# Value products three loop steps behind the scores, a third probability buffer, and a rewritten tail, in an attention and expert kernel on one core

## The chip, the core and the metric

The kernel runs on one core of one Trainium2 chip. The metric is the time on the device in microseconds (us) of one execution of the program. Engines are called by the names of the profile: PE (TensorE matmuls), PEld (its weight loads), DVE (VectorE), ACT (ScalarE), POOL (GpSimd) and SP (SyncE, which here only starts transfers).

## The reference, cut to what matters

Two sequences of 1024 tokens of 256 numbers pass through a cross attention with 16 heads over 64 keys and then through a mixture of 16 experts of which each token takes two, with a capacity of 320 rows for an expert.

```python
x = x + tanh(g_xattn) * attention(layernorm(x), ctx, ...)   # q@k, mask, softmax over 64 keys, @v, @Wo + bo
x = x + tanh(g_ffn) * experts(layernorm(x), gate_w, w1, w2)

# inside experts, for 2048 tokens:
probs = sigmoid(xf @ gate_w.T);  top_vals, sel = top_k(probs, 2)
weights = top_vals / (top_vals.sum(-1, keepdims=True) + 1e-06)
ranks = running count of each expert, token by token, minus 1
slot = where(ranks < 320, sel * 320 + ranks, none)          # rows past the capacity are dropped
h = gelu(padded @ w1[e]);  out_rows = h @ w2[e]             # one expert after the other
out = sum over the two choices of out_rows[slot] * weight
```

The count runs over all tokens in order, so the last tile's rows can be placed only when every tile before it has been counted, and the experts begin only when all rows are placed.

## The kernel before, in words

The program is written out by hand for each engine: five instruction streams, which meet at semaphores. An engine runs its own stream strictly in the written order, so an instruction that waits holds all behind it.

There are three parts. First the weights are prepared: the key side is folded into the query weights and the value side into the output weights, through a list of jobs (`JOBS`), of which the last eight make the folded value weights. Then comes the loop over 16 tiles of 128 tokens, 0 to 15. Last come the 16 experts.

The loop is a software pipeline (`steps`, from s = -2 to 15). In one step s, PE does in this order:

- it turns (transposes) the probabilities of tile s-2 into the PSUM tile `ps_pT` (`turn_probs`, L1217)
- it makes the scores of tile s in two halves (`score`, L1234 and L1240)
- it turns the residual rows of tile s-3 (`turn_x1`, L1248)
- it makes the value products of tile s-2, 24 matmuls into `ps_out` (`attend`, L1269), with the router's product of tile s-3 in the middle (`router`, L1256)
- in every second step it makes the counts of a pair of tiles (`counts`, L1283 to L1286), and while there are tiles left it turns the normalised input two tiles ahead (L1326).

Around it, DVE takes the row minima of the scores, subtracts them ("centres" the first eight heads, L937), sums the exponentials, makes the low part of the turned probabilities (L848, in the tail L968), adds the residual (L873, in the tail L978), and does the routing: sigmoid, the two largest, their places, the counts and the slot of each row (`slot_row`, L879, in the tail L1023). ACT makes the exponentials (L636, L640), the high part of the turned probabilities (L606), copies the turned residual rows (L622), scales the rows that are sent to the experts (`second_rows`, L615) and makes the gate's exponentials (`gate_exp`, L630). POOL splits the normalised input (L483, L484), normalises the probabilities (L492), makes the second layer norm's factor of a tile (`second_norm`, L468 to L470) and sends each tile's rows to their slots by two indirect transfers (`dispatch`, L460).

A pair r is tiles 2r and 2r+1, so pairs 5, 6 and 7 are tiles 10 to 15. Behind the last loop step all engines go through a tail that is written out tile by tile. There PE runs dummy matmuls at four places (`keep_busy`, L1193): 5 and 3 between attention work, and 40 ahead of the first expert's turned rows (L1354) and 8 behind them. When POOL has sent the last rows it writes `sent` (L540), and SP, once all transfers of rows have landed (L369), fetches the first expert's rows (L378).

Of the kernel before, what the change touches and what calls it, by code (L numbers as in the profile page):

```python
# [19 lines left out]
TILES = TOKENS // P  # L20
PER_BATCH = SEQ // P
# [54 lines left out]
def build(nc, x, ctx_in, mask, g_xattn, g_ffn, ln_gamma, ln_beta, wq, wkv, wo, bo, gate_w, w1, w2, out):  # L76
# [8 lines left out]
    with ExitStack() as held:  # L85
# [65 lines left out]
        probs = sb("probs", [P, 2, HEADS, KEYS])  # L151
# [5 lines left out]
        kv_rows = probs[:, :, :, :].rearrange("p a n k -> p a (n k)")  # L157
# [4 lines left out]
        l2 = sb("l2", [P, 2, 3])  # L162
        eps_c = sb("eps_c", [P, 1])
# [63 lines left out]
        ps_attn = ps_out[:, 0:DIM]  # L227
# [36 lines left out]
        gated_read = sem("gated_read")  # L264
# [26 lines left out]
        JOBS_AFTER = {-2: range(N_FIRST, N_FIRST + 4), -1: range(N_FIRST + 4, N_KEYS + 4), 0: range(N_KEYS + 4, N_JOBS)}  # L291
# [10 lines left out]
        LAST = TILES - 1  # L302
        LATE_PAIR = PAIRS - 3
        CONSTS = 7
# [97 lines left out]
        def _(pool):  # L402
# [60 lines left out]
            def second_norm(t):  # L463

                p = t % 2
                pool.wait_ge(stats2_ready, t + 1)
                wait(pool, z2_ready, t - 1)
                done.done(pool.tensor_tensor(l2[:, p, 0:1], mv2[:, p, 1:2], eps_c[:, :], ALU.add))  # L468
                done.done(pool.tensor_tensor(l2[:, p, 1:2], l2[:, p, 0:1], power[:, 0:1], ALU.pow))
                pool.tensor_scalar(l2[:, p, 2:3], mv2[:, p, 0:1], l2[:, p, 1:2], -1.0, ALU.mult, ALU.mult).then_inc(ln2_ready, 1)  # L470

            def step(s, j, i):
# [14 lines left out]
                def normalise():  # L487

                    t, p = s - 1, (j + 1) % 2
                    if exists(t):  # L490
                        pool.wait_ge(norm_ready, t + 1)
                        pool.tensor_tensor(probs[:, p], probs[:, p], norm[:, p, :, None].to_broadcast([P, HEADS, KEYS]),  # L492
                                           ALU.mult).then_inc(normed, 1)

                if 1 <= s <= 2:
                    normalise()
                    split()
                else:
                    split()
                    if exists(s - 3) and s < LAST:  # L500
                        second_norm(s - 3)
                    normalise()
                    if s == LAST:
                        second_norm(s - 3)
# [6 lines left out]
                r = i - 3  # L511
                if exists(r, PAIRS) and s < LAST:
                    if j == 0:
# [4 lines left out]
                    dispatch(r, j)  # L518
                    if s == LAST - 1:
                        dispatch(r, 1)  # L520
# [3 lines left out]
            mark_tokens(PAIRS - 3)  # L524
            pool.wait_ge(slots_ready, PAIRS - 2)
# [35 lines left out]
        def _(act):  # L561
# [82 lines left out]
            def step(s, j, i):  # L644
# [29 lines left out]
                if exists(s):  # L674
                    probs_exp(s)
# [767 lines left out]
```

## Time and profile before

| quantity | value |
|---|---|
| time, median of 3 runs | 340.29 us (338.02 to 340.69) |
| the profiled execution: its own time | 339.9 us |
| the profiled execution: its span | 338.2 us |
| mean granted TensorE clock | 0.968 of full speed |
| PE busy | 308.3 us, 91% |
| DVE, ACT, POOL busy | 251.2, 207.9, 191.4 us |
| PE: value products (L1269) | 384 matmuls, 289 ns each by the mean |
| POOL: indirect transfers of rows (L460) | 32, 1043 ns each |

The span is the time from the first to the last instruction of the profiled execution; 1.7 us of its own time lie outside. In a timeline row, the number behind the start is how long the engine was busy with the group of instructions, and the brackets at its end say how long the engine had been idle ahead of it and what ended that. A busy PE is not a PE at its peak: a matmul's busy time overlaps with the next one's, so the pace is read from the distance of starts. The loop lies between about 33 and 156 us of the span, the tail of the attention part between 156 and 178, the experts from 186 to the end.

### The profile page before, as it was taken

To read this page: it belongs to the slowest core of one execution; us is meant where nothing else is said; L and a number is where in the kernel's file an instruction comes from. 1 tells how busy PE (TensorE), PEld (TensorE's weight loads), DVE (VectorE), ACT (ScalarE), POOL (GpSimd) and SP (SyncE) were. 2 spreads that over 40 slices of the span, in tenths; PEclk is the share of its full clock that TensorE was granted. 3 is DMA by queue.
4 is the path that set the end of the run, shared out by engine and by line. 5 is a ranking of instruction groups with operands and counts; after the bars stand their busy time and mean duration, and the time that the engine had idled before them with its cause. 6 is when DMAs were issued, how large, how long until landed. Compare 5 with 4: busy or idle time off the path is not lost. (4 is left out here: it accounts for less than half of the span.)

```text
span 338.2 us, 6265 instructions
## 1 busy us (share of the span) xinstructions
PE 308.3 (91%) x2077; PEld 267.3 (79%) x2080; DVE 251.2 (74%) x585; ACT 207.9 (61%) x570; POOL 191.4 (57%) x242
## 2 busy tenths in 40 slices
PE   8989999999999999998849999999999999999800
PEld 3646779988888888887724899999999999999700
DVE  2679887698989898989755398888888888887200
ACT  2646877887888888866461376666666666665300
POOL 8034566585777777788771023555555555566650
PEclk9999999999999999999978999999999999999965
DMA  6989999700111111111224737878787878853440
GB/s 159 274 241 292 182 167 152 195 19 16 49 49 55 57 57 64 56 51 62 78 95 149 249 104 201 204 205 208 204 216 211 224 202 220 211 82 43 48 46 8
DMA packets 40906, 45.68 MB, mean 135 GB/s; under 512 B 5461, under 2 KB 34666, under 8 KB 40874
## 3 DMA queue, kind: packets, MB, share of 16 engines
q1 hardware_dynamic: 33410, 35.78, 39.3%
q0 software_dynamic: 7424, 9.48, 15.6%
q8 instruction: 17, 0.28, 0.4%
q14 instruction: 15, 0.12, 0.2%
q10 hardware_dynamic: 40, 0.02, 0.0%
HBM read 28.02 MB, written 17.24 MB: 134 GB/s over the span
## 5 line engine op out<-in xcount | busy, mean ns | idle before, releaser
L554 POOL DMA_INDIRECT out_dram<-wqT,diag x48 | 73.3, 1528 | 77.4 <-DMA out_dram<-wqT,diag 43.4
L1370 PE MATMUL ps_scores<-value_t,score_t 128*128 128x320 f32 x384 | 59.1, 310 | 0.0
L1370 PEld LDWEIGHTS ps_scores<-value_t,score_t 128*128 128x128 f32 x384 | 56.5, 188 | 0.4 <-DVE value_t L1079 0.3
L1269 PE MATMUL ps_out<-value_t,pT 128*128 128x256 f32 x384 | 53.3, 289 | 0.9 <-DVE pT L968 0.9
L1240 PE MATMUL ps_scores<-score_t,xn 128*128 128x512 f32 x192 | 53.9, 426 | 0.0
L1269 PEld LDWEIGHTS ps_out<-value_t,pT 128*128 128x128 f32 x384 | 47.7, 189 | 1.7 <-issue 1.6
L1240 PEld LDWEIGHTS ps_scores<-score_t,xn 128*128 128x128 f32 x192 | 36.4, 190 | 6.8
L713 ACT ACTIVATE ps_scores<-ps_scores 128x640 f32<-128x640 f32 x30 | 20.6, 688 | 34.2 <-PE ps_scores L1370 34.1
L460 POOL DMA_INDIRECT padded<-z,slot_row x32 | 33.4, 1043 | 10.0 <-issue 7.1
L640 ACT ACTIVATE probs<-ps_scores,row_low 128x64 f32<-128x64 f32 x128 | 38.0, 327 | 0.5 <-DVE row_low L941 0.5
L1093 DVE CAST value_t<-ps_scores 128x640 fp32r<-128x640 f32 x30 | 24.7, 824 | 18.0 <-ACT ps_scores L713 17.8
L492 POOL TENSOR_TENSOR probs<-probs,norm 128x1024 f32<-128x1024 f32 x15 | 28.6, 1906 | 5.5 <-DVE norm L909 5.5
L640 ACT ACTIVATION_READ_ACCUMULATOR probs<-ps_scores,row_low 128x1 f32 x128 | 28.4, 222 | 0.0
L848 DVE TENSOR_TENSOR pT<-ps_pT,pT 128x512 fp32r<-128x512 f32 x28 | 18.5, 660 | 5.2 <-ACT pT L606 4.9
L1095 DVE TENSOR_TENSOR value_t<-ps_scores,value_t 128x512 fp32r<-128x512 f32 x30 | 20.8, 692 | 1.0
L1106 DVE TENSOR_TENSOR score_t<-raw,score_t 128x1024 fp32r<-128x1024 f32 x16 | 19.4, 1216 | 2.6 <-POOL sent L540 2.6
L1193 PE MATMUL ps_misc<-zeros 128*128 128x512 bf16 x62 | 18.8, 461 | 1.5 <-DVE zeros L805 1.2
L1079 DVE TENSOR_TENSOR value_t<-ps_pT,value_t 128x640 fp32r<-128x640 f32 x16 | 13.1, 816 | 8.2 <-ACT value_t L701 8.2
L606 ACT ACTIVATE pT<-ps_pT 128x512 fp32r<-128x512 f32 x32 | 18.0, 644 | 0.9 <-PE ps_pT L1217 0.9
L701 ACT ACTIVATE value_t<-ps_pT 128x640 fp32r<-128x640 f32 x16 | 11.3, 706 | 11.9 <-PE ps_pT L1354 11.7
L630 ACT ACTIVATE gexp<-ps_scores,l 128x16 f32<-128x16 f32 x16 | 4.4, 276 | 22.3 <-PE ps_scores L1256 16.7
L483 POOL CAST xn<-xn_full 128x256 fp32r<-128x256 f32 x16 | 6.4, 399 | 20.6 <-ACT xn_full L654 20.5
(210 smaller groups left out, 690.0 us busy)
## 6 DMA issues: line engine op xcount, KB each, us to landing
raw<-in_L_ffn_w_dram SPq DMA_DIRECT2D x16, 512.0 KB, 4.8
wo_sb<-in_L_ffn_w_dram SPq DMA_DIRECT2D x16, 512.0 KB, 3.5
padded<-empty SPq DMA_DIRECT2D x2, 2064.0 KB, 31.0
diag<-padded SPq DMA_DIRECT2D x16, 258.0 KB, 4.9
out_dram<-x SPq DMA_DIRECT2D x16, 128.0 KB, 1.7
padded<-empty SPq DMA_DIRECT2D x1, 1032.0 KB, 34.1
diag<-padded SPq DMA_DIRECT2D x16, 64.5 KB, 4.7
wq_sb<-in_L_xattn_Wq_dram SPq DMA_DIRECT2D x2, 512.0 KB, 8.0
```

The source lines that it names most:

```text
L460: pool.indirect_dma_start(padded, bass.IndirectOffsetOnAxis(ap=slot_row[:, r % 2, k, q:q + 1], axis=0), z2[:, (2 * r + k) % RING, q], None ...
L492: pool.tensor_tensor(probs[:, p], probs[:, p], norm[:, p, :, None].to_broadcast([P, HEADS, KEYS]), ALU.mult).then_inc(normed, 1)
L554: pool.indirect_dma_start(out, bass.IndirectOffsetOnAxis(ap=xg[0:SLOTS[k], r, k, TOKEN:TOKEN + 1].bitcast(U32), axis=0), y[0:SLOTS[k], j, ...
L640: op = act.activation(probs[:, j, n], ps_scores[:, 1, at:at + KEYS], ACT.Exp, scale=-1.0, bias=row_low[:, n:n + 1], accum_out=row_sum[:, j ...
L713: act.activation(h_at(t, h), ps_scores[:, 2 * h:2 * h + 2, 0:CAPACITY], ACT.Gelu).then_inc(h_act, 1)
L1093: dve.tensor_copy(h_high_of(p)[:, fs], h_at(t, h)).then_inc(h_high, 1)
L1095: dve.tensor_tensor(h_low_of(p)[:, fs], h_at(t, h)[:, :, 0:n], h_high_of(p)[:, fs, 0:n].bitcast(F32), ALU.subtract)
L1106: dve.tensor_tensor(w1_hl(p, 1), raw1[:, p], w1_hl(p, 0).bitcast(F32), ALU.subtract).then_inc(w1_low, 1)
L1193: pe.matmul(ps_misc[:, :], idle_rows[:, 0:P], idle_rows, start=True, stop=True)
L1240: op = pe.matmul(dst, xn[:, t % 2, a, c], mv, start=False, stop=last)
L1269: op = pe.matmul(ps_attn, pT[:, a, c], mv, start=c == 0 and (a, b) == PARTS[0], stop=c == HC - 1 and (a, b) == PARTS[-1])
L1370: op = pe.matmul(ps_scores[:, f, 0:CAPACITY], w1_hl(p, a)[:, c, f * P:(f + 1) * P], x_hl(p, b)[:, c], start=c == 0 and (a, b) == PARTS[0], ...
```

## The change

All work on a tile behind its scores moves one step back in the loop: probabilities of tile s-3 are turned in step s, the residual rows of tile s-4 are turned, and so on. For that `probs` has three buffers in place of two (`DEEP = 3`). The eight value jobs are spread 3, 2 and 3 over the steps -1, 0 and 1, where they were 4 and 4 over -1 and 0.

Behind the last scores, the probabilities of the next tile are turned ahead of the value products of a tile. For this the value products of tiles 13 and 15 go to `ps_misc` and not to `ps_out`, and their turned probabilities go to a part of `score_t` that is no longer read. The turned residual rows and the router's product are put between matmuls of the next tile's value products, in place of the 5 and 3 dummies. The 40 and 8 dummies ahead of the experts stay.

In the tail, the second layer norm of tiles 12 to 15 leaves POOL with the power alone; DVE adds two small instructions and ACT one per tile (`shift`). The routing step that stood in the last loop step for pair 5 is now in the tail. Two waits are loosened, so that products of tile 13 need not wait for the residual of tile 12. The core of the diff (the loop's shift by u = s-1 repeats on every engine):

```diff
-        probs = sb("probs", [P, 2, HEADS, KEYS])
+        probs = sb("probs", [P, DEEP, HEADS, KEYS])
+        pT_late = score_t[:, 6 * 1024:].rearrange("p (k c n) -> p k c n", k=2, c=HC)
-        ps_attn = ps_out[:, 0:DIM]
+        def attn_of(t):
+            return ps_misc[:, 0:DIM] if t in (LAST - 2, LAST) else ps_out[:, 0:DIM]
+        def pT_of(t, k):
+            return pT_late[:, k] if t in (LAST - 2, LAST) else pT[:, k]
...
+        VALUES_AFTER = {0: range(N_KEYS + 3, N_KEYS + 5), 1: range(N_KEYS + 5, N_JOBS)}
+        LATE_TILE = 2 * LATE_PAIR + 2
@@ GpSimd: second_norm, and the tail
+                if t >= LATE_TILE:
+                    pool.tensor_tensor(l2[:, p, 1:2], l2[:, p, 0:1], power[:, 0:1], ALU.pow).then_inc(ln2_ready, 1)
+                    return
...
             mark_tokens(PAIRS - 3)
+            normalise(LAST)
+            mark_tokens(PAIRS - 2)
             pool.wait_ge(slots_ready, PAIRS - 2)
-            dispatch(PAIRS - 3, 0, (0,))
+            dispatch(PAIRS - 3, 0)
+            second_norm(LAST - 3)
+            dispatch(PAIRS - 3, 1, (0,))
             second_norm(LAST - 2)
-            dispatch(PAIRS - 3, 0, (1,))
-            dispatch(PAIRS - 3, 1)
-            mark_tokens(PAIRS - 2)
+            dispatch(PAIRS - 3, 1, (1,))
             mark_tokens(PAIRS - 1)
             second_norm(LAST - 1)
             pool.wait_ge(slots_ready, PAIRS - 1)
             dispatch(PAIRS - 2, 0)
+            second_norm(LAST)
             dispatch(PAIRS - 2, 1)
-            second_norm(LAST)
@@ ScalarE: the tail
+            copy_probs(LAST - 2)
+            later_exp(LAST, 8, 12)
+            gate_exp(LAST - 4)
+            later_exp(LAST, 12, HEADS)
+            second_rows(LAST - 4)
             copy_probs(LAST - 1)
+            copy_x1(LAST - 3)
+            gate_exp(LAST - 3)
+            copy_probs(LAST)
+            second_rows(LAST - 3)
             copy_x1(LAST - 2)
-            second_rows(LAST - 3)
             gate_exp(LAST - 2)
             second_rows(LAST - 2)
-            copy_probs(LAST)
             copy_x1(LAST - 1)
+            gate_exp(LAST - 1)
             second_rows(LAST - 1)
-            gate_exp(LAST - 1)
@@ VectorE: the tail
+            low_probs(LAST - 2, 0)
+            low_probs(LAST - 2, 1)
             dve.wait_ge(exped0, TILES)
...
-            place(PAIRS - 3, 0, 2, PAIRS - 2)
-            first_residual(LAST - 2)
-            second_stats(LAST - 2)
+            begin(PAIRS - 3, 0, 2)
+            find(0, 2)
             dve.wait_ge(exped1, TILES)
...
-            dve.tensor_tensor(probs[:, p], probs[:, p], norm[...], ALU.mult).then_inc(normed, 1)
+            first_residual(LAST - 3)
+            link.sync()
+            choose(PAIRS - 3, 0, 2)
+            low_probs(LAST - 1, 0)
+            low_probs(LAST - 1, 1)
+            weigh(PAIRS - 3, 0, 2)
+            counts_of(PAIRS - 3)
+            place(PAIRS - 3, 0, 2, PAIRS - 2)
+            second_stats(LAST - 3)
+            first_residual(LAST - 2)
+            second_stats(LAST - 2)
+            low_probs(LAST, 0)
+            low_probs(LAST, 1)
+            first_residual(LAST - 1)
             begin(PAIRS - 2, 0, 2)
             find(0, 2)
+            second_stats(LAST - 1)
             link.sync()
             choose(PAIRS - 2, 0, 2)
...
             place(PAIRS - 2, 0, 2, PAIRS - 1)
+            first_residual(LAST)
+            second_stats(LAST)
@@ TensorE: the last step and the tail
+                if s == LAST:
+                    turn_probs(LAST - 2)
...
             turn_probs(LAST - 1)
-            turn_x1(LAST - 2)
-            keep_busy(5)
-            attend(LAST - 1, {HC // 2: lambda: router(LAST - 2)})
+            attend(LAST - 2, {1: lambda: turn_x1(LAST - 3), HC - 3: lambda: router(LAST - 3), HC - 1: lambda: counts(PAIRS - 3)})
             turn_probs(LAST)
+            attend(LAST - 1, {2: lambda: turn_x1(LAST - 2), HC - 2: lambda: router(LAST - 2)})
+            attend(LAST, {2: lambda: turn_x1(LAST - 1), HC - 2: lambda: router(LAST - 1)})
             counts(PAIRS - 2)
-            turn_x1(LAST - 1)
-            keep_busy(3)
-            attend(LAST, {HC // 2: lambda: router(LAST - 1)})
             turn_x1(LAST)
+            router(LAST)
             count_one(0)
-            router(LAST)
             count_one(1)
```

What this makes of three streams is best seen in the order of the instructions. Line numbers of the change are its own.

On TensorE, ahead of the value products of the tile behind the loop's last one, before (the products are those of tile 14, L1217 turns probabilities, L1248 residual rows):

```order
L1217 MATMUL ps_pT<-ident,probs 128x128 x8
L1248 MATMUL ps_scores<-ident,x 128x128 x2
L1193 MATMUL ps_misc<-zeros 128x512 x5
L1269 MATMUL ps_out<-value_t,pT 128x256 x12
L1256 MATMUL ps_scores<-small_t,wq_sb 128x16 x2
L1269 MATMUL ps_out<-value_t,pT 128x256 x12
L1217 MATMUL ps_pT<-ident,probs 128x128 x8
```

and in the change, from the turned probabilities of tile 14 on (L1271; L1323 are value products of tile 13, L1302 turned residual rows of tile 12, L1310 the router, L1337 and L1340 counts):

```order
L1271 MATMUL ps_pT<-ident,probs 128x128 x8
L1323 MATMUL ps_misc<-value_t,score_t 128x256 x3
L1302 MATMUL ps_scores<-ident,x 128x128 x2
L1323 MATMUL ps_misc<-value_t,score_t 128x256 x12
L1310 MATMUL ps_scores<-small_t,wq_sb 128x16 x2
L1323 MATMUL ps_misc<-value_t,score_t 128x256 x6
L1337 MATMUL ps_scores<-running,ones_b 128x16
L1340 MATMUL ps_scores<-both,before 128x16
```

The dummies are gone, and the residual rows of one tile are turned behind the first three products of the next.

On GpSimd, from the last normalised probabilities of the loop on, before (L468 to L470 are the second layer norm, first of tile 12, then of tile 13; L460 sends rows of pair 5):

```order
L492 TENSOR_TENSOR probs<-probs,norm 128x1024
L468 TENSOR_TENSOR l<-mv,eps_c 128x1
L469 TENSOR_TENSOR l<-l,power 128x1
L470 TENSOR_SCALAR l<-mv,l 128x1
L453 TENSOR_TENSOR z<-token,zeros 128x4
L460 DMA padded<-z,slot_row 32768x258
L468 TENSOR_TENSOR l<-mv,eps_c 128x1
L469 TENSOR_TENSOR l<-l,power 128x1
L470 TENSOR_SCALAR l<-mv,l 128x1
L460 DMA padded<-z,slot_row 32768x258 x3
```

and in the change (L492 normalises tile 15's probabilities, L473 sends rows of pair 5, L481 is the power of the second layer norm, of tile 12 and then of tile 13):

```order
L466 TENSOR_TENSOR z<-token,zeros 128x4
L492 TENSOR_TENSOR probs<-probs,norm 128x1024
L466 TENSOR_TENSOR z<-token,zeros 128x4
L473 DMA padded<-z,slot_row 32768x258 x2
L481 TENSOR_TENSOR l<-l,power 128x1
L473 DMA padded<-z,slot_row 32768x258
L481 TENSOR_TENSOR l<-l,power 128x1
L473 DMA padded<-z,slot_row 32768x258
```

The factor of tile 12 stood ahead of every transfer of pair 5; it now stands behind two of them.

On ScalarE in the tail, before, from the turned probabilities of tile 15 (L606) on (L622 copies the turned residual rows of tile 14, L615 scales that tile's rows, L630 is its gate):

```order
L606 ACTIVATE pT<-ps_pT 128x512 x2
L622 ACTIVATE wq_sb<-ps_scores 128x256
L615 ACTIVATE z<-x,l 128x2x256
L630 ACTIVATE gexp<-ps_scores,l 128x16
```

and in the change, from the turned probabilities of tile 14 (L625) on (L646 copies residual rows of tile 12, L654 is the gate's exponential of tile 12, then come tile 15's turned probabilities, the scaled rows of tile 12, and the residual rows of tile 13):

```order
L625 ACTIVATE pT<-ps_pT 128x512 x2
L646 ACTIVATE wq_sb<-ps_scores 128x256
L654 ACTIVATE gexp<-ps_scores,l 128x16
L625 ACTIVATE score_t<-ps_pT 128x512 x2
L635 ACTIVATE shift<-l 128x1
L639 ACTIVATE z<-x,shift,l 128x2x256
L646 ACTIVATE wq_sb<-ps_scores 128x256
```

The gate's exponential of tile 12 now stands ahead of the turned probabilities of tile 15 and of the residual rows of tile 13.

## Rows read from the trace of the kernel before

**Rows 1.** Windows: length, busy (count) of PE, PEld, DVE, ACT, POOL; clock, DMA share, GB/s.
```profile
57.00:148.00 91.00, 90.75 (x650) 81.26 (x649) 77.75 (x225) 71.82 (x284) 67.67 (x102) 1.00 0.21 61
...
174.00:178.00 4.00, 3.00 (x10) 1.11 (x11) 1.72 (x12) 3.99 (x5) 2.76 (x4) 0.50 0.29 100
```

**Rows 2.** Timeline of TensorE, the last step: start us, busy us, engine, line, operation.
```profile
144.18 0.38 PE L1248 MATMUL ps_scores<-ident,x 128*128 128x128 f32 x2
...
147.69 1.04 PE L1217 MATMUL ps_pT<-ident,probs 128*128 128x128 f32 x8
...
148.56 0.38 PE L1234 MATMUL ps_scores<-mask_b,ident_b 128*128 128x512 bf16 x1
...
151.76 0.38 PE L1248 MATMUL ps_scores<-ident,x 128*128 128x128 f32 x2
```

**Rows 3.** Timeline of the start: TensorE's one wait, then GpSimd.
```profile
47.79 0.39 PE L1234 MATMUL ps_scores<-mask_b,ident_b 128*128 128x512 bf16 x1 [0.59 <-ACT probs L640]
...
48.00 0.24 POOL L444 TENSOR_SCALAR ln_nb<-ln_a 128x4 f32<-128x4 f32 x1
...
49.87 1.91 POOL L492 TENSOR_TENSOR probs<-probs,norm 128x1024 f32<-128x1024 f32 x1 [1.63 <-DVE norm L909]
...
52.20 0.73 POOL L484 TENSOR_TENSOR xn<-xn_full,xn 128x256 fp32r<-128x256 f32 x1
```

**Rows 4.** Timeline of TensorE behind the last scores, to the first expert.
```profile
156.96 0.44 PE L1248 MATMUL ps_scores<-ident,x 128*128 128x128 f32 x2 [0.42 <-DVE x L978]
...
158.86 1.66 PE L1269 MATMUL ps_out<-value_t,pT 128*128 128x256 f32 x12 [0.39 <-DVE pT L968]
...
165.67 1.66 PE L1269 MATMUL ps_out<-value_t,pT 128*128 128x256 f32 x12 [0.47 <-DVE pT L968]
...
175.02 0.18 PE L1295 MATMUL ps_scores<-both,before 128*128 128x16 bf16 x1
...
180.12 6.21 PE L1193 MATMUL ps_misc<-zeros 128*128 128x512 bf16 x28 [0.22 <-issue]
...
186.18 0.86 PE L1354 MATMUL ps_pT<-ident,diag 128*128 128x128 f32 x6
```

**Rows 5.** Timeline of GpSimd behind the last scores.
```profile
158.23 0.57 POOL L469 TENSOR_TENSOR l<-l,power 128x1 f32<-128x1 f32 x1
...
166.70 1.06 POOL L460 DMA_INDIRECT padded<-z,slot_row  x1 [0.39 <-issue]
...
177.42 0.96 POOL L460 DMA_INDIRECT padded<-z,slot_row  x1 [0.30 <-issue]
```

**Rows 6.** Timeline of VectorE: one centring in the loop, then the tail.
```profile
144.38 0.69 DVE L937 TENSOR_TENSOR probs<-ps_scores,row_low 128x512 f32<-128x512 f32 x1
...
161.27 0.18 DVE L991 TENSOR_SCALAR gden<-gexp 128x32 f32<-128x32 f32 x1 [0.82 <-ACT gexp L630]
...
162.87 0.23 DVE L1007 TENSOR_TENSOR chosen<-iota_f,top_i 128x64 bf16<-128x64 f32 x1
...
166.01 0.16 DVE L1023 SCALAR_TENSOR_TENSOR slot_row<-top_i,rank 128x4 uint32<-128x4 uint32 x1
...
169.39 0.48 DVE L978 SCALAR_TENSOR_TENSOR x<-ps_out,tgates,x_all 128x256 f32<-128x256 f32 x1 [0.18 <-PE ps_out L1269]
...
173.20 0.21 DVE L991 TENSOR_SCALAR gden<-gexp 128x16 f32<-128x16 f32 x1 [1.14 <-ACT gexp L630]
```

**Rows 7.** Timeline of ScalarE behind the last scores.
```profile
156.86 1.13 ACT L606 ACTIVATE pT<-ps_pT 128x512 fp32r<-128x512 f32 x2
...
161.13 0.81 ACT L615 ACTIVATE z<-x,l 128x512 f32<-128x512 f32 x1
...
164.80 0.38 ACT L622 ACTIVATE wq_sb<-ps_scores 128x256 f32<-128x256 f32 x1 [0.84 <-PE ps_scores L1248]
...
172.82 0.27 ACT L630 ACTIVATE gexp<-ps_scores,l 128x16 f32<-128x16 f32 x1 [2.02 <-POOL l L470]
```

**Rows 8.** Timeline of SyncE: the first fetch of an expert's rows.
```profile
180.19 0.38 SPq L378 DMA_DIRECT2D diag<-padded  x1
```

More of the change, by code:

```diff
@@ L20 @@
 TILES = TOKENS // P
+LAST = TILES - 1
+DEEP = 3
 PER_BATCH = SEQ // P
@@ L162, in build @@
         l2 = sb("l2", [P, 2, 3])
+        shift = sb("shift", [P, 2, 1])
         eps_c = sb("eps_c", [P, 1])
@@ L499, in step @@
                     split()
[L500 to L504, printed above, removed]
+                    if exists(u - 3):
+                        second_norm(u - 3)
+                    if exists(s - 1):
+                        normalise(s - 1)
                 if s == 1:
@@ L612, in second_rows @@
                 act.wait_ge(ln2_ready, t + 1)
+                bias = l2[:, p, 2:3]
+                if t >= LATE_TILE:
+                    bias = shift[:, p]
+                    act.activation(bias, l2[:, p, 2:3], ACT.Copy, scale=l2[:, p, 1:2]).then_inc(shifted, 1)
+                    act.wait_ge(shifted, t - LATE_TILE + 1)
                 if t >= RING:
@@ L1259, in attend @@
             def attend(t, between):
-                wait(pe, x1_ready, t)
+                wait(pe, x1_ready, t if t < LAST - 2 else t - 1)
                 for c in range(HC):
@@ L1268, in attend @@
                         mv = value_w[b][:, batch_of(t), c]
-                        op = pe.matmul(ps_attn, pT[:, a, c], mv, start=c == 0 and (a, b) == PARTS[0],
+                        op = pe.matmul(attn_of(t), pT_of(t, a)[:, c], mv, start=c == 0 and (a, b) == PARTS[0],
                                        stop=c == HC - 1 and (a, b) == PARTS[-1])
@@ L1305, in step @@
                     score(s, 1)
-                if exists(s - 3):
-                    turn_x1(s - 3)
-                r = i - 2
-                counted_here = j == 1 and exists(r, PAIRS)
-                between = {}
-                if exists(s - 3):
-                    between[HC // 2] = lambda: router(s - 3)
-                if counted_here and r >= LATE_PAIR:
-                    between[HC - 2] = lambda: counts(r)
-                if exists(s - 2):
-                    attend(s - 2, between)
-                if counted_here and r < LATE_PAIR:
-                    counts(r)
+                if exists(u - 3):
+                    turn_x1(u - 3)
+                if s == LAST:
+                    turn_probs(LAST - 2)
+                if exists(u - 2):
+                    attend(u - 2, {HC // 2: lambda: router(u - 3)} if exists(u - 3) else {})
+                if ju == 1 and exists(iu - 2, PAIRS):
+                    counts(iu - 2)
                 t = s + 2
```

152 lines of the change are left out of this document (78 added, 74 removed).

## The prediction

> **What bounds the kernel now.** I read the busy shares by stretches first, to see which parts can gain at all. In the loop, from 57 to 148 us, PE is busy for 90.75 of 91 us at full clock [rows 1]. So one more step of distance between scores and products cannot shorten a loop step; it can only move work between the start, the loop and the tail. Then I read PE's timeline at both ends. At the start it has one wait, 0.59 us [rows 3]. In the tail there are two holes, filled in part by dummies: the residual rows of tile 13 are turned at 156.96 and the products of tile 14 begin at 158.86; those of tile 15 begin at 165.67 after a similar hole [rows 4]. Together that is about 4 us. Last I read what the tail's end hangs on. The last count ends on PE at 175.2; then PE runs its 40 dummies without a pause, 28 of them from 180.12 to 186.3, and the first expert's rows are turned at 186.18 [rows 4]. The transfers end at 178.38 on POOL [rows 5] and SP fetches at 180.19 [rows 8]. So two paths meet at 186.18: **the last count plus 11.1 us of dummies**, and **the last transfer plus 1.8 us plus the landing of a fetch**. The turned rows follow the dummies without a gap, so the first path decided and the second was no later. From there the experts run on PE, untouched by the change, and I take them as shifted whole.
>
> **Loop and start.** Taken out of the loop ahead of the last step is one tile's later half: turned probabilities 0.87 us (147.69 to 148.56) and residual rows, products and router 3.51 us (144.18 to 147.69) [rows 2]. The last step would begin 4.38 us earlier, at 143.3. PE is idle more at the start, though: with no products to do, it reaches the fourth tile's scores by about 50. Their split input stands on POOL behind the first norms (end 48.24), one normalisation (1.91) and the split (1.2 with its cast), thus at 50.5 to 51.4, the norms starting up to 0.9 earlier with the lighter value jobs; in the kernel before the split ended at 52.93 [rows 3]. That is 0.5 to 1.4 us of waiting where 0.59 us stood before, and the exponentials, now with less PE work to hide them, cost some tenths more. I take 0.8 us net (0 to 1.5). The last step then begins at 144.1.
>
> **The tail, link by link.** Times are estimates on the old trace's time axis. Small DVE instructions, whose rows are not shown one by one, count 0.2 us each (161.27 and 173.20 took 0.18 and 0.21) [rows 6].
>
> - PE: scores of tile 15 end at 144.1 + 0.87 + 3.20 = 148.2 [rows 2]; residual rows 0.14, turned probabilities of tile 13 0.87, products of tile 12 3.4: 152.6; turned probabilities of tile 14: 153.5.
> - DVE: in the loop the centring ends at 144.38 + 0.69, 0.9 us behind the residual rows of its step at 144.18 [rows 2, 6]; these stand at 148.2 in the last step, so it ends at 149.1. ACT: exponentials of a copy's size 0.6, copies for tile 13 1.13 [rows 7]; DVE's low parts end at 151.4. A row sum (of the centring's size, 0.7), then gate and places of pair 5, which took 161.27 to 162.87, 1.6 us [rows 6], the reciprocal and norm (0.5) and the residual of tile 12 (0.48): **154.7**. PE reached the place for tile 12's residual rows at 153.9 and waits 0.9 us.
> - PE then has 18 products and the router ahead of the counts of pair 5, of the 3.37 us that 24 and the router take [rows 2], and DVE four small instructions to their slots: 158.6.
> - POOL may now send pair 5. The order puts two transfers, 1.27 us each (0.96 busy and 0.30 of issue) [rows 5], ahead of tile 12's power (0.57): 161.9. In the old kernel even tile 13's power ended at 158.8 [rows 5], with tile 12's ahead of it.
> - ACT holds at the gate's exponential of tile 12 until then, as it did for 2.02 us at 172.82 [rows 7], and behind it in its queue stand tile 15's copies (1.1), the new `shift` (0.3 with its wait, bounded by the cheapest ACT row, 0.27, and twice that), scaled rows (0.81) and tile 13's residual rows (0.38) [rows 7]: 164.7.
> - PE reached the router of tile 13 at 161.7 and waits **3.1 us**, longer than either old hole. Rest of tile 14's products: 166.1.
> - DVE: residual and statistics of tile 14 (0.9, two of the residual's size), gate and places of pair 6 (1.6), the statistics' end (0.4, of which the two added instructions make 0.1 to 0.2 each), choice, weights and counts to slots (1.8, nine small ones): slots of pair 6 at 170.8. They were there at 166.17 [rows 6].
> - DVE goes on: residual of tile 15 begins at 171.0, against 169.39 [rows 6]; statistics until 172.3. From a tile's gate to its count took 1.82 us, 173.20 to 175.02 [rows 4, 6], and to its slots four small ones more: tile 14 until 175.0. Tile 15's gate to count 1.82: the last count ends at **177.0, against 175.2: +1.8 us**. In the old kernel a wait of 1.14 us for the gate stood in that stretch [rows 6]; it goes, since ACT has the gates in time.
> - POOL: eight transfers from 170.9 at 1.27 and one power at 0.67: end at 181.7, against 178.38: +3.3 us. Fetch at 183.5. A fetch before took under 6.0 us (180.19 to 186.18), so it lands between 186.5, if 3 us suffice, and 189.5.
>
> The first path gives 177.0 + 11.1 = 188.1, the second at most 189.5. I take the first with a tenth for the second: the experts begin at 188.2, **+2.0 us**. The profiled execution took 339.9 us by itself (span 338.2 and 1.7 around it), so its like is 341.9. The median of the runs is 0.4 above it, so I forecast **342.3 us**. Costed at nothing: the third buffer, the second homes, the loosened waits (they only allow); the DVE and POOL work of the loop, which is covered by 90.75 us of PE; the weight loads for the experts, which SP issues behind the fetches and which would be late only if the experts began much before them.
>
> **The rivals.**
>
> *The dropped clock (slower).* In the old tail PE, after a thin stretch behind the last products, ran at half clock: 0.50 in 174 to 178 [rows 1]. The old holes of about 2 us had dummies in them. The change takes these out and makes, by my sum, a hole of 3.1 us with nothing in it. If the clock falls there, the 30 products behind the hole go at half speed. Here 12 products with a busy 1.66 us follow each other at about 0.125. Dummies of 512 columns went 28 in 6.21 us at full clock, 0.22 each [rows 4]; at half clock that is 0.44, and a product of half the columns 0.22 at least. So 0.09 more for each of 30 is 2.7 us, all on the path to the last count: **345.0 us**. For: the old drop. Against: that drop came after a longer thin stretch, and work stands on both sides of this hole. The Trainium skill, "TensorE: Matmul & The Clock Gate", section "HAM oscillation — how this bites in real kernels", says that a wait between two bursts can send the next burst cold each time. By that rule 345.0 would be the sum; the old trace agrees only for the longer stretch.
>
> *The holes are filled as written (faster).* If ACT does not stand at tile 12's gate, PE saves 4 us of holes less 0.8 at the start, and DVE and POOL follow: about **337.3 us**. It decides from the point at which tile 12's power comes before about 158.5, for then the router's rows are there in time. Against: POOL's order is fixed, and the two transfers ahead of the power wait themselves for slots at 158.6.
>
> *Dummies shorter.* If the clock is up when the 40 dummies run, they take about 8.8 us and not 11.1, and the fetch decides. With a landing in 3 to 4 us that is +0.5 to +1.5: **341.3 us**. For: the clock's phase is open. Against: PE is nearly idle ahead of the dummies in the change too.
>
> *Fetch and queue late.* If the landing takes all of 6 us and the waits at each link are a tenth longer, +4: **344.3 us**.
>
> **How the numbers follow.** My case as summed, 0.46; dropped clock 0.22; shorter dummies 0.15; late fetch 0.09; filled holes 0.08. The likeliest gives 342.3, with its own range of 341.0 to 343.8 from the start's 0 to 1.5 and the fetch. The range for 8 in 10 runs from 339.2 to 345.8: it takes in all but most of the filled holes and the upper part of the clock's case. A measurement of this kernel tells about 1% from no change, 3.4 us, so faster is below 336.9 and slower above 343.7. Faster: about half of the filled holes lies below 336.9, 0.05 with rounding. Slower: nearly all of the dropped clock, half of the late fetch and a tenth of my own case, 0.31. Within 1%: 0.64.
>
> **What would show each step.** The last tile's scores should begin 3 to 4.4 us earlier; if not, the start's sum is wrong. On ACT, one gate's exponential should stand behind a wait of over 5 us for the power on POOL, and PE should wait about 3 us for copied residual rows in tile 14's products; if it waits under 1 us there, the filled holes are right. The granted clock in that stretch decides the second case. The last transfer should end about 3 us later than 178.4 and the last count about 2 us later than 175.2. If the first expert's rows are turned behind a wait, the fetch decided, and not the dummies. A loop in which PE is idle by more than some tenths would overturn all of it.

## The result and the profile after

The changed kernel takes 345.61 us by the median of 4 runs (344.20 to 346.76), beside 339.93 for the kernel before (4 runs, 338.02 to 340.69). The ratio is 1.018 with a 95% interval of 1.015 to 1.0209: 5.7 us slower by the medians and 6.1 by the ratio, where 342.3 was forecast in a range of 339.2 to 345.8. The profiled execution took 346.72 us by itself, its span is 345.0, its mean granted clock 0.956 (0.968 before). All comparisons below are ratios with their interval; they leave disturbed runs out, so they can differ from the quotient of two medians.

The loop and its two ends in windows of the profile after (length, busy time and count of PE, PEld, DVE, ACT, POOL, then granted clock, DMA share, GB/s):

```profile
27.00:57.00 30.00, 27.89 (x138) 20.81 (x137) 25.72 (x65) 21.80 (x84) 17.92 (x30) 1.00 1.12 201
57.00:148.00 91.00, 91.00 (x644) 81.11 (x643) 77.98 (x230) 72.71 (x290) 65.48 (x99) 1.00 0.15 51
163.00:165.00 2.00, 0.00 (x0) 0.00 (x0) 1.14 (x2) 1.90 (x5) 1.64 (x3) 1.00 0.27 99
...
167.00:167.50 0.50, 0.50 (x6) 0.50 (x5) 0.38 (x1) 0.50 (x1) 0.00 (x0) 1.00 0.04 8
167.50:168.00 0.50, 0.50 (x6) 0.43 (x4) 0.47 (x3) 0.17 (x1) 0.00 (x0) 0.53 0.00 0
168.00:170.50 2.50, 2.50 (x14) 2.50 (x13) 2.19 (x17) 0.38 (x1) 0.49 (x1) 0.50 0.15 52
171.00:174.00 3.00, 1.37 (x15) 1.24 (x16) 1.52 (x8) 1.27 (x3) 0.67 (x1) 1.00 0.00 0
175.00:184.00 9.00, 5.59 (x19) 2.57 (x20) 4.81 (x30) 6.54 (x9) 7.16 (x9) 0.50 0.31 108
```

The same window of the start in the kernel before:

```profile
27.00:57.00 30.00, 28.96 (x150) 22.67 (x149) 26.26 (x68) 22.40 (x82) 16.59 (x29) 1.00 1.12 192
```

In the start, 27 to 57 us, PE is idle for 2.11 us; in the kernel before it was 1.04. The loop is as full as before [rows 1]. Then come two stretches at 0.50. The second answers to the one of before; the first, with PE busy in all of it, is new. It begins at about 167.5 and ends at about 170.9.

PE's timeline of the same kernel, from the last scores to the first expert (start, busy time, engine, line, operation, and in brackets the idle time ahead and what ended it); it answers to [rows 2, 4]:

```profile
144.64 0.38 PE L1288 MATMUL ps_scores<-mask_b,ident_b 128*128 128x512 bf16 x1
...
160.79 1.67 PE L1323 MATMUL ps_out<-value_t,pT 128*128 128x256 f32 x12
165.66 0.62 PE L1310 MATMUL ps_scores<-small_t,wq_sb 128*128 128x16 f32 x4 [3.20 <-ACT wq_sb L646]
...
168.00 2.91 PE L1323 MATMUL ps_misc<-value_t,score_t 128*128 128x256 f32 x12
...
172.10 0.17 PE L1340 MATMUL ps_scores<-both,before 128*128 128x16 bf16 x1
...
179.48 0.17 PE L1349 MATMUL ps_scores<-both,before 128*128 128x16 bf16 x1
179.50 11.30 PE L1247 MATMUL ps_misc<-zeros 128*128 128x512 bf16 x40
190.64 0.86 PE L1400 MATMUL ps_pT<-ident,diag 128*128 128x128 f32 x6
```

The last scores begin 3.9 us earlier (144.64 against 148.56). The hole ahead of the router of tile 13 is 3.20 us. The 12 products at 160.79 take 1.67 us, the same 12 at 168.00 take 2.91. The last count is 4.4 us later than before, and so is the first expert: 190.64 against 186.18, again directly behind the dummies.

What held PE: ScalarE and GpSimd of the profile after, answering to [rows 5, 7].

```profile
163.06 0.27 ACT L654 ACTIVATE gexp<-ps_scores,l 128x16 f32<-128x16 f32 x1 [6.03 <-POOL l L481]
163.24 1.07 ACT L625 ACTIVATE score_t<-ps_pT 128x512 fp32r<-128x512 f32 x2
164.19 0.30 ACT L635 ACTIVATE shift<-l 128x1 f32<-128x1 f32 x1
164.53 0.81 ACT L639 ACTIVATE z<-x,shift,l 128x512 f32<-128x512 f32 x1
165.25 0.36 ACT L646 ACTIVATE wq_sb<-ps_scores 128x256 f32<-128x256 f32 x1
```

```profile
160.16 1.01 POOL L473 DMA_INDIRECT padded<-z,slot_row  x1 [2.48 <-issue]
161.47 0.96 POOL L473 DMA_INDIRECT padded<-z,slot_row  x1 [0.30 <-issue]
162.46 0.57 POOL L481 TENSOR_TENSOR l<-l,power 128x1 f32<-128x1 f32 x1
...
173.33 1.04 POOL L473 DMA_INDIRECT padded<-z,slot_row  x1 [2.76 <-DVE slot_row L1065]
...
182.81 0.96 POOL L473 DMA_INDIRECT padded<-z,slot_row  x1 [0.30 <-issue]
```

The chain is the one of the prediction: two transfers, the power, the gate behind a wait of 6.03 us, four instructions, and then PE. The last transfer ends at 183.77, 5.4 us later than before.

At the end of the run, the last three additions into the output (POOL, L571) of the changed kernel:

```profile
331.01 1.56 POOL L571 DMA_INDIRECT out_dram<-wqT,diag  x1 [2.42 <-issue]
332.87 1.56 POOL L571 DMA_INDIRECT out_dram<-wqT,diag  x1 [0.31 <-issue]
334.74 1.43 POOL L571 DMA_INDIRECT out_dram<-wqT,diag  x1 [0.30 <-issue]
```

and in the kernel before PE's last product and the first of the last three additions (L554):

```profile
320.62 0.28 PE L1399 MATMUL ps_scores<-score_t,value_t 128*128 128x256 f32 x1
324.07 1.56 POOL L554 DMA_INDIRECT out_dram<-wqT,diag  x1 [2.40 <-issue]
```

PE's last product ends at 325.7, 4.8 us later than before (320.9), but the last three additions begin 6.9 us later (331.01 against 324.07). Of the 6.8 us between the two profiled executions, 4.5 lie ahead of the first expert, 0.3 in PE's work on the experts and 2.0 in this queue. The medians differ by 5.7.

### The profile page after: what moved, and what is told of

It is laid out like the page before. It is cut to its first block and busy times, and to the rows that moved or that the text cites. A ratio compares the mean times of both kernels' runs of the same rounds, so it can differ in the third digit from the quotient of the medians.

```text
span 345.0 us, 6252 instructions
## 1 busy us (share of the span) xinstructions
PE 309.5 (90%) x2072; PEld 268.5 (78%) x2072; DVE 250.8 (73%) x592; ACT 208.8 (61%) x574; POOL 191.2 (55%) x235
## 5 line engine op out<-in xcount | busy, mean ns | idle before, releaser
L571 POOL DMA_INDIRECT out_dram<-wqT,diag x48 | 74.3, 1547 | 78.0 <-DMA out_dram<-wqT,diag 35.1
L1323 PE MATMUL ps_out<-value_t,pT 128*128 128x256 f32 x336 | 46.7, 288 | 0.0
L1323 PEld LDWEIGHTS ps_out<-value_t,pT 128*128 128x128 f32 x336 | 41.8, 189 | 0.1
L473 POOL DMA_INDIRECT padded<-z,slot_row x32 | 32.3, 1010 | 13.4 <-issue 9.2
L492 POOL TENSOR_TENSOR probs<-probs,norm 128x1024 f32<-128x1024 f32 x16 | 30.5, 1905 | 3.2 <-DVE norm L945 3.1
L666 ACT ACTIVATION_READ_ACCUMULATOR probs<-ps_scores,row_low 128x1 f32 x128 | 28.4, 222 | 0.0
L884 DVE TENSOR_TENSOR pT<-ps_pT,pT 128x512 fp32r<-128x512 f32 x26 | 17.2, 660 | 6.5 <-ACT pT L625 6.0
L654 ACT ACTIVATE gexp<-ps_scores,l 128x16 f32<-128x16 f32 x16 | 4.4, 275 | 26.9 <-PE ps_scores L1310 15.6
L736 ACT ACTIVATE value_t<-ps_pT 128x640 fp32r<-128x640 f32 x16 | 11.3, 705 | 12.5 <-PE ps_pT L1400 12.4
L1247 PE MATMUL ps_misc<-zeros 128*128 128x512 bf16 x57 | 17.4, 472 | 1.2 <-DVE zeros L840 1.2
L758 ACT ACTIVATE score_t<-raw 128x1024 fp32r<-128x1024 f32 x16 | 16.8, 1056 | 0.3
```

The costliest lines, as they stand in the source:

```text
L473: pool.indirect_dma_start(padded, bass.IndirectOffsetOnAxis(ap=slot_row[:, r % 2, k, q:q + 1], axis=0), z2[:, (2 * r + k) % RING, q], None ...
L492: pool.tensor_tensor(probs[:, p], probs[:, p], norm[:, t % 2, :, None].to_broadcast([P, HEADS, KEYS]), ALU.mult).then_inc(normed, 1)
L571: pool.indirect_dma_start(out, bass.IndirectOffsetOnAxis(ap=xg[0:SLOTS[k], r, k, TOKEN:TOKEN + 1].bitcast(U32), axis=0), y[0:SLOTS[k], j, ...
L666: op = act.activation(probs[:, t % DEEP, n], ps_scores[:, 1, at:at + KEYS], ACT.Exp, scale=-1.0, bias=row_low[:, n:n + 1], accum_out=row_s ...
L1247: pe.matmul(ps_misc[:, :], idle_rows[:, 0:P], idle_rows, start=True, stop=True)
L1323: op = pe.matmul(attn_of(t), pT_of(t, a)[:, c], mv, start=c == 0 and (a, b) == PARTS[0], stop=c == HC - 1 and (a, b) == PARTS[-1])
```

## The experiments

### The hole and the clock

**e1**, the hole filled with dummies:

```diff
-            attend(LAST - 1, {2: lambda: turn_x1(LAST - 2), HC - 2: lambda: router(LAST - 2)})
+            def fill_then_router():
+                pe.wait_ge(x1_ready, LAST - 1)
+                keep_busy(14)
+                router(LAST - 2)
+            attend(LAST - 1, {2: lambda: turn_x1(LAST - 2), HC - 2: fill_then_router})
```

> The changed kernel, with 14 dummies (3.1 us at 0.22 each) put into the 3.20 us hole in tile 14's products, ahead of the router of tile 13. Theory A (the clock fell because of the empty hole): the granted clock stays at 1.00 from 166 to 172, the products of tile 15 take 1.7 us for 12 and not 2.91, the counts of pair 6 come 1.3 us earlier and the whole is 1.3 us shorter, about 344.3. Theory B (the clock falls for another reason, or DVE's chain sets the counts anyway): the time stays at 345.6.

Measured: ratio 1.0063 (1.0043 to 1.0083), so 1.17% or 4.0 us faster than the changed kernel (2.8 to 5.2 with both intervals taken in). TensorE in e1, and two windows of it:

```profile
161.07 3.19 PE L1247 MATMUL ps_misc<-zeros 128*128 128x512 bf16 x14
164.42 0.62 PE L1310 MATMUL ps_scores<-small_t,wq_sb 128*128 128x16 f32 x4 [0.16 <-ACT wq_sb L646]
...
176.81 0.18 PE L1349 MATMUL ps_scores<-both,before 128*128 128x16 bf16 x1
176.84 10.10 PE L1247 MATMUL ps_misc<-zeros 128*128 128x512 bf16 x40
186.77 0.86 PE L1406 MATMUL ps_pT<-ident,diag 128*128 128x128 f32 x6
```

```profile
161.00:172.00 11.00, 8.87 (x63) 6.48 (x62) 6.70 (x32) 5.75 (x14) 5.23 (x9) 1.00 0.13 48
173.00:179.00 6.00, 2.42 (x10) 1.01 (x11) 4.18 (x27) 5.35 (x8) 4.60 (x6) 0.50 0.25 89
```

PE does not get on sooner, it only works at something, and the clock stays at 1.00. Theory A holds for the clock, and for its price up to the last count (1.3 expected). The whole gained more than that. The experts begin 3.87 us earlier than in the profile after. Of that, 0.5 is there at the last scores already (they begin at 144.14). Another 0.8 of it lies ahead of the router of tile 12: in the profile after, ACT stood 1.59 us between its two copies for tile 14, and here it did not. Neither of these is the work of the dummies. From the router of tile 13 to the last count it is 1.4 less (12.4 us here, 13.8 there); in e3 and e4 below, where the work at this place also ran at 1.00, it is 12.4 and 12.3. That 1.4 is the price of the dropped clock.

The last 1.2 lies in the 40 dummies, which take 9.9 us from first start to the expert, against 11.1. They begin inside the second stretch at 0.50, and 2.7 us of them lie in it here, 5.1 in the profile after. That this hangs on the hole is not shown. In e3 and e4 there is no drop behind the hole, and yet the second stretch lasts 10.2 us, as in the profile after (6.8 in e1), and the 40 dummies take 11.48 and 11.25 us up to the first expert. Their dummies, first e3, then e4 and its first expert:

```profile
174.99 11.65 PE L1247 MATMUL ps_misc<-zeros 128*128 128x512 bf16 x40
...
174.00 11.41 PE L1247 MATMUL ps_misc<-zeros 128*128 128x512 bf16 x40
185.25 0.86 PE L1400 MATMUL ps_pT<-ident,diag 128*128 128x128 f32 x6
```

**e2**, the hole made longer; **e3**, made shorter on ACT:

```diff
@@ e2, GpSimd
             dispatch(PAIRS - 3, 0)
-            second_norm(LAST - 3)
             dispatch(PAIRS - 3, 1, (0,))
+            second_norm(LAST - 3)
@@ e3, ScalarE
-            gate_exp(LAST - 3)
             copy_probs(LAST)
-            second_rows(LAST - 3)
             copy_x1(LAST - 2)
+            gate_exp(LAST - 3)
+            second_rows(LAST - 3)
```

> The changed kernel, with one more transfer (1.27 us) ahead of tile 12's power on POOL. Theory A (POOL's order holds ACT, ACT's copies hold PE): ACT waits 7.3 us at tile 12's gate and not 6.03, PE's hole is 4.5 us and not 3.20, and all that follows is 1.3 us later or, with more of the products at half clock, up to 2.3: 346.9 to 347.9. Theory B (the hole is not on the path to the end): 345.6.

Measured for e2: ratio 1.0215 (1.0175 to 1.0254), 0.35% or 1.2 us over the changed kernel's, with overlapping intervals. In its profile the first expert begins at 192.16, 1.5 us later than in the changed kernel's.

> The changed kernel, with tile 15's copies and the copy of tile 13's residual rows ahead of tile 12's gate in ACT's queue; PE's router of tile 13 still waits for that gate. Theory A: the hole ends with the gate at 163.4 and not at 165.66, so it shrinks to about 1 us, the clock stays up, and the end is 2.2 us earlier for the hole and 1.3 for the clock: 342.1. If the hole counts but the clock does not: 343.4. Theory B (neither is on the path): 345.6.

Measured for e3: ratio 1.0123 (1.0071 to 1.0175), 1.9 us faster than the changed kernel (0.2 to 3.7 by its own interval; with the changed kernel's taken in as well, from nothing to 4.0), where theory A had 3.5. Four of its six runs took 341.8 to 342.4, the other two 345.7 and 346.7; the median is 342.32. The row of the router in e2, then a window of e2:

```profile
166.31 1.04 PE L1310 MATMUL ps_scores<-small_t,wq_sb 128*128 128x16 f32 x4 [4.46 <-ACT wq_sb L646]
```

```profile
166.00:172.00 6.00, 5.69 (x26) 5.69 (x27) 2.83 (x17) 1.91 (x5) 0.25 (x1) 0.50 0.12 44
```

The hole is 4.46 us as written ahead of the run, and now the work behind it is at half clock from its first product up to 172.2. In e3, the router and a window with the hole in it:

```profile
162.61 0.59 PE L1310 MATMUL ps_scores<-small_t,wq_sb 128*128 128x16 f32 x4 [1.01 <-ACT gexp L654]
```

```profile
160.00:170.00 10.00, 7.18 (x61) 6.56 (x59) 7.08 (x34) 4.61 (x12) 6.29 (x9) 1.00 0.22 79
```

The hole is 1.01 us, where about 1 was expected, and does not lower the clock. The last count comes at 175.1 and the first expert at 186.47, 4.2 us before the changed kernel's. The direction is theory A's; the interval is too wide to tell whether the clock's part is in the time.

**e10**, the kernel before without the dummies in its holes:

```diff
-            keep_busy(5)
             attend(LAST - 1, {HC // 2: lambda: router(LAST - 2)})
...
-            keep_busy(3)
             attend(LAST, {HC // 2: lambda: router(LAST - 1)})
```

> The kernel before, without the 5 and 3 dummies in the two holes of its tail, so that two holes of about 2 us stand empty. Theory A1 (only an empty stretch as long as the changed kernel's 3.20 us drops the clock): granted clock 1.00 up to 170, no change, 339.9. Theory A2 (two holes of 2 us are enough): the clock falls to 0.50 somewhere in 159 to 170 and the products there take twice as long, 341 to 343.

Measured: ratio 1.004 (1.0009 to 1.0071). The two holes, and the windows of both:

```profile
158.11 1.66 PE L1269 MATMUL ps_out<-value_t,pT 128*128 128x256 f32 x12 [1.46 <-DVE pT L968]
...
164.92 1.67 PE L1269 MATMUL ps_out<-value_t,pT 128*128 128x256 f32 x12 [0.91 <-DVE pT L968]
```

```profile
155.00:163.00 8.00, 5.88 (x51) 5.16 (x49) 6.59 (x27) 5.07 (x17) 6.24 (x9) 1.00 0.19 66
163.00:171.00 8.00, 5.25 (x39) 4.46 (x38) 6.26 (x28) 2.07 (x5) 5.75 (x11) 1.00 0.28 99
```

The clock stays up over both, as A1 said; the time is 1.4 us longer all the same (0.3 to 2.4), which neither said. In this profile the last count ends at 174.45, the experts begin at 185.81 and PE's last product ends at 320.6, all a little earlier than before; but the last three additions begin at 325.86, 5.3 us behind PE and not 3.2. So this profile is longer at the end, and why stays open. For the granted clock, then, it was not enough that the change took dummies out; the hole it made was also longer than these two.

### The order of the tail

**e4**, tile 12's power early (DVE and POOL):

```diff
             low_probs(LAST - 1, 0)
+            second_stats(LAST - 3)
             low_probs(LAST - 1, 1)
...
-            second_stats(LAST - 3)
@@ GpSimd
+            second_norm(LAST - 3)
             pool.wait_ge(slots_ready, PAIRS - 2)
             dispatch(PAIRS - 3, 0)
-            second_norm(LAST - 3)
```

> The changed kernel, with tile 12's statistics on DVE between the two low parts of tile 14 and its power on POOL ahead of the wait for the slots of pair 5. Theory A: ACT no longer waits over 1 us at tile 12's gate, PE's hole of 3.20 us goes, the clock stays at 1.00, and the slots of pair 6 stand at about 168 and not 173; the whole is 4.5 us shorter: 341.1. Theory B (the loss of 5.7 us lies in the longer sending and the dummies, not in the hole): at most 1.5 us shorter, 344.1 or more.

Measured: ratio 1.0017 (0.9983 to 1.005), 5.5 us faster than the changed kernel. In its profile, ACT's gate of tile 12 and PE's router of tile 13:

```profile
158.78 0.28 ACT L654 ACTIVATE gexp<-ps_scores,l 128x16 f32<-128x16 f32 x1 [2.90 <-POOL l L481]
```

```profile
161.71 0.52 PE L1310 MATMUL ps_scores<-small_t,wq_sb 128*128 128x16 f32 x4
```

No hole is left in front of the router, and moving one small chain gives back all of the loss, within the interval. From the last scores to the last count the profile is 5.9 us shorter than the changed kernel's (29.1 against 35.0): 3.2 for the hole, 1.4 for the clock, 0.8 for the pause on ACT, and 0.5 in other places.

**e7** goes on from e4: tile 13's power behind two of pair 5's transfers, tile 13's residual rows copied ahead of tile 12's scaled rows, and the counts of pair 6 ahead of PE's last three products. **e11** puts DVE's gates of pair 6 ahead of tile 14's residual as well, and on PE takes tile 14's residual rows two places later and the last router behind the counts of pair 6; **e12** is e11 with 36 dummies. The part of e11 on DVE:

```diff
@@ e11 over e7, VectorE
-            first_residual(LAST - 1)
             begin(PAIRS - 2, 0, 2)
             find(0, 2)
-            second_stats(LAST - 1)
+            first_residual(LAST - 1)
             link.sync()
             choose(PAIRS - 2, 0, 2)
+            second_stats(LAST - 1)
```

> The changed kernel with the tail reordered: tile 12's statistics and power early as in the run before, tile 13's power after two of the four transfers of pair 5, the copy of tile 13's residual rows ahead of tile 12's scaled rows, and the counts of pair 6 ahead of tile 15's last three products on PE. Theory A (the tail's order alone made the loss): no hole over 1 us, slots of pair 6 at about 167 (before: 166.17), last count at about 174 and last transfer at about 178: the level of the kernel before or 1 us under it, 339 to 340. Theory B (the third step of distance costs in the loop or the start too): 341 or more.

> The reordered tail of run e7, with one more change: DVE takes the gates of pair 6 ahead of tile 14's residual (it stood idle for 1.20 us ahead of that one while the gates were ready), and PE takes tile 14's residual rows two steps later in tile 15's products, then the counts of pair 6 and last the router. Theory A (the tail's order sets the sending, and the sending the end): slots of pair 6 at 166.5 against 168.0, last transfer 1.5 us earlier, experts at about 184 since the 40 dummies stay, and 338.5 to 339.5, level with the kernel before or just under it. Theory B (PE's work after the last scores is what bounds): nothing over e7, 340.1.

> The same with 36 dummies ahead of the first expert and not 40: at 0.22 us each 0.9 us less. Theory A (the dummies end last): the experts begin 0.9 us earlier, 337.6 to 338.6. Theory B (the fetch of expert 0 ends last by then): the same time as the run before.

Measured: 1.0024 (0.9998 to 1.0051), 1.0007 (0.9967 to 1.0047) and 1.0001 (0.9961 to 1.0042). All three are level with the kernel before, none beats it. Yet in their profiles the experts begin at 184.66, 184.57 and 183.97, up to 2.2 us before [rows 4]. The last additions of e12:

```profile
326.74 1.56 POOL L570 DMA_INDIRECT out_dram<-wqT,diag  x1 [2.36 <-issue]
328.60 1.56 POOL L570 DMA_INDIRECT out_dram<-wqT,diag  x1 [0.31 <-issue]
330.47 1.43 POOL L570 DMA_INDIRECT out_dram<-wqT,diag  x1 [0.30 <-issue]
```

PE's last product ends at 319.0 there, but these begin 7.7 us later; in the kernel before it was 3.2. The queue loses this over all the experts: its first addition comes 2.2 us earlier than in the kernel before (198.45 against 200.63), its last three begin 2.7 us later. In the profiled executions, then, an earlier start of the experts is given back in that queue. How much of it in the others is open: the profiled one of e12 took 342.41 us and that of e11 342.58, where the medians of the compared runs are 339.4 and 339.5.

### Between the last count and the end

**e5** is the kernel before with `keep_busy(60)` in place of 40; **e6** is the changed kernel with `keep_busy(30)`.

> The kernel before, with 60 dummies ahead of the first expert and not 40: at 0.22 each 4.4 us more, so that the experts begin where they begin in the changed kernel (190.6). Theory A (the start of the experts passes to the end whole, and nothing else of the change is lost): 339.9 + 4.4 = 344.3, or above by what the queue of the final additions adds. Theory B (part of the start's shift is given back, or transfers already bind the experts): clearly less than 344.3, 342 or so.

> The changed kernel, with 30 dummies ahead of the first expert and not 40. The last 10 take 2.2 us at full clock. Theory A (the dummies end last by 1.8 us, the fetch of expert 0 landing 3.5 us behind its issue, at 188.8): the experts begin 1.8 us earlier, 343.8. Theory B (fetch and dummies end together): no change, 345.6. If fewer dummies leave the clock down for the first expert: 345.6 or more.

e5: ratio 1.0136 (1.0107 to 1.0165), 4.6 us over the kernel before, near the 4.4 of theory A. In the profiles the shift is smaller: its experts begin at 189.16, 3.0 us later than before and not 4.4, and its profiled execution took 342.81 us against 339.9, 2.9 more. A later start of the experts passes to the end.

e6: ratio 1.0186 (1.0138 to 1.0233), no different from the changed kernel's. But its eight executions scatter from 342.7 to 362 us, the profiled one took 356.21, and the three shortest took 342.66, 343.71 and 345.18; the middle one is at theory A's 343.8. In its profile the experts begin 2.0 us earlier than in the changed kernel's, at 188.65, behind a wait of 0.72 us for the fetch. Whether these 2.0 us reach the end stays open.

**e8** and **e9**, the kernel before and the changed one with two additions per expert and not three:

```diff
                     if k == SLOT_TILES - 1:
                         pool.wait_ge(y_last, e + 1)
+                        continue
```

(the waits for `added` count 2 * 16 in place of 3 * 16). Both leave the rows of slots 256 and up out of the output.

> The kernel before, without the third addition of each expert (the rows of slots 256 and up are left out of the output, nothing else is). The queue of the additions then has a third less to do. Theory A (this queue, and not PE, ends the run, 2.0 us behind PE's pace in the trace of before and 4.5 us in that of the change): the last addition follows PE's last product within 1.5 us, and the time falls by 2 to 4 us, to 336 to 338. Theory B (PE's pace ends the run): only the last addition itself is saved, 1.9 us: 338.

> The changed kernel, without the third addition of each expert, as in the run before. Theory A (of the 5.7 us, 4.4 lie in the later start of the experts and 1.3 in the queue of the additions): the difference to the run before shrinks to 4.4 us or a little under. Theory B (the rest lies elsewhere in the experts): it stays at 5.7.

Measured: e8 0.9838 (0.9825 to 0.9851), e9 1.0008 (0.9985 to 1.0031). The last additions, of e8 and of e9:

```profile
320.28 1.55 POOL L555 DMA_INDIRECT out_dram<-wqT,diag  x1 [3.25 <-ACT wqT L730]
```

```profile
326.72 1.55 POOL L572 DMA_INDIRECT out_dram<-wqT,diag  x1 [3.47 <-DMA out_dram<-wqT,diag]
```

PE's last product ends at 319.88 and 326.15, so the queue now follows PE by 0.4 and 0.6 us. It does end the run in both kernels, and was worth 5.5 and 5.8 us, more than the 2 to 4 expected. But the difference between the kernels stays: 1.70%, 5.8 us. Theory A of e9 is out, and the number of theory B is right: the queue took no part in the loss, and the 2.0 us of it between the two profiled executions are what one execution differs from another. But theory B looked for the rest in the experts, and there it is not: from the first expert to PE's last product it is 134.8 us in e8 and 135.0 in e9. The loss is in the start of the experts: 185.13 in e8, 191.13 in e9. The profiles of before, e10 and e8 have it at 186.18, 185.81 and 185.13, those of after and e9 at 190.64 and 191.13: the middle ones are about 5.1 apart.

## Why the prediction was wrong

**The mechanism was right, the case chosen was not.** ACT stands behind tile 12's power (over 5 us forecast, 6.03 measured), PE waits at tile 13's router (3.1 and 3.20), and only the last scores gain (3.6 forecast, 3.9). The step that failed is the likeliest case's granted clock: it let the products behind the hole go at full speed, and gave the dropped clock a chance of 0.22. The argument against it was that "work stands on both sides of this hole". The trace shows why this is no argument: PE resumes at 165.66 and the clock falls about 2 us later, in the midst of the work. e1, which changes only what PE does in the hole, keeps the clock there; 1.4 us of its gain are that clock.

The clock alone does not make up the miss. The last count came 2.6 us later than forecast. In round numbers 1.4 is the clock, 0.8 the pause on ACT, for which I had no term, 0.8 links that I had too short, and 0.3 came back because the last scores began earlier than forecast. The rival of the dropped clock has a sum, 345.0, that is 0.6 off the median, but this is partly luck. Its price for one product held (12 took 2.91 us and not 1.67, 0.10 more each, where I had 0.09). But the clock was back at 170.9, so only about half of the 30 products were slow, and the 2.7 us of the rival were 1.4; the pause and the short links stood in for the rest.

The Trainium skill, "TensorE: Matmul & The Clock Gate", section "HAM oscillation — how this bites in real kernels", says that a wait between bursts makes the next one start cold. e2 agrees: the work behind its 4.46 us starts at 0.50. In the profile after, the work behind 3.20 us started at 1.00 and went cold only on the way. Holes of 1.01 us in e3 and of 1.46 and 0.91 us in e10 had no such effect.

**The links.** Counted from the last scores, the forecast has the slots of pair 5 after 13.6 us, the copy for tile 13 after 19.7, the slots of pair 6 after 25.8 and the last count after 32.0. In the profile after it was 14.8, 21.0, 28.4 and 35.0; in e1, with the clock up and without the 1.59 us pause on ACT, the last count came after 32.8. So 0.8 is the sum of my short links, and the other 2.2 are clock and pause.

**The start.** The loss was forecast at 0.8 us; PE's idle time from 27 to 57 rose by 1.07, and by up to 1.13 in the other kernels with this loop. The profile of before is also a late one. Its last scores begin at 148.56, those of e8, e10 and e5, which have the same loop, at 147.87, 147.81 and 148.03. Measured against e8 the gain is 3.2 us, not 3.9. That fits medians which differ by more than the 4.5 us between the two profiles.

**Right as written:** the loop gains nothing; the first expert follows the dummies and not the fetch; the 40 dummies took 11.1 us in both, which was luck, since they took from 9.9 (e1) to 11.5 us (e3) in kernels that differ from the changed one in a few instructions; the last transfer and the last count are both late (3.3 and 1.8 forecast, 5.4 and 4.4 measured). **The experts "shifted whole"** holds for PE, and e5 shows it for a later start. For an earlier one it does not: e7, e11 and e12 gained up to 2.2 us there in the profile and nothing in the time. So my 337.3 for filled holes was wrong as well: e7 has no hole over 1.2 us before the last count's chain and takes 340.2, 1.0024 of before.

## What to carry to other kernels

Price a hole on TensorE by its length and by the work behind it: an empty 3.20 us brought the clock down some 2 us after work had resumed, which cost 1.4 us up to the last count, and single holes of 1.5 us or less amid work did not. Dummies in the long one gave back 4.0 of the 6.1 us, by the ratios, but only 1.4 of this can be traced to them. The length of one hole does not decide by itself: in e4 the clock fell at 169.1, behind a wait of 1.63 us and with little work after it. When a tail is reordered, follow each small instruction that other engines wait for (here one power of 0.57 us) past every transfer put ahead of it; moving it back was worth the whole loss. Before counting on an earlier start of the last phase, look whether its end hangs on another queue, as the additions here, which run up to 7.7 us behind PE.

## What the runs showed of the hardware

- The granted clock lags what PE does: in the profile after it fell about 2 us after work had begun again, and it stayed down for 3.4 us with PE busy throughout. Behind the same hole it fell 1.8 us after work had begun in e9 (at 168.0) and 0.7 us after in e6 (at 166.2). In e2, behind 4.46 us of idling, it was down from before the work resumed until 172.
- ACT stood for 1.59 us between two copies of the same tile in the profile after, with the turned probabilities there since 153.3; the trace names only "remote" as what ended it. It stood likewise in e6 (1.57), e7 (1.56), e11 (1.62), e12 (1.86) and e9 (0.96); in e1, e2, e3 and e4 the copies follow each other. What it is stays open; by the comparison with e1 it cost PE about 0.8 us:

```profile
156.16 0.60 ACT L625 ACTIVATE pT<-ps_pT 128x512 fp32r<-128x512 f32 x1 [1.59 <-remote]
```

- Three indirect additions per expert end the run, not PE: leaving one of three out saves 5.5 us of 339.3 in the kernel before. Why they fall behind PE by 3.2 us in one profile and 7.7 in another was not settled.
